# A decoder layer in float32 on one core: the softmax's row sums move from GpSimd and TensorE to ScalarE's accumulator, and VectorE writes the rounded query and key projections

## The reference

```
qkv = x @ attn_qkvw + attn_qkvb                      # q, k, v: 2 x 32 heads x 512 x 32
scores = einsum('bhqd,bhkd->bhqk', q, k) * (1 / sqrt(32))
probs = softmax(scores, axis=-1)
ctx = einsum('bhqk,bhkd->bhqd', probs, v)
x = layernorm(x + ctx @ attn_ow + attn_ob)
x = layernorm(x + fake_quant(x) @ fake_quant(ctx_4096))       # 1024 x 1024 per batch
x = layernorm(x + x @ W_base.T + b_base + experts(x))         # top 2 of 8 experts of rank 16
```

## Time and profile before

| | us |
|---|---|
| median of 3 runs | 793.83 (792.41 to 796.04) |
| profiled execution, span | 793.7 |
| TensorE (PE) busy | 745.3, 94% |
| VectorE (DVE) busy | 516.9, 65% |
| ScalarE (ACT) busy | 284.9, 36% |
| GpSimd (POOL) busy | 443.0, 56% |

### The profile page before, as it was taken

How to read it: one execution, slowest core, us unless ns; L and a number is a source line. 1 busy time by engine, 2 the same in 40 slices (tenths; PEclk the granted TensorE clock), 3 DMA queues, 4 the chain that set the end, 5 groups by cost and what they waited for, 6 DMA issues and landing times.

```text
span 793.7 us, 11643 instructions
## 1 busy us (share of the span) xinstructions
PE 745.3 (94%) x3688; PEld 533.3 (67%) x3688; DVE 516.9 (65%) x791; ACT 284.9 (36%) x443; POOL 443.0 (56%) x323
## 2 busy tenths in 40 slices
PE   5989999999999999999999998779999977999996
PEld 4758667668668668668667663257766756788884
DVE  4766558558558558558558567875667679466554
ACT  3214334334334334334334354613443481211111
POOL 4056597497587587587587467823453374112111
PEclk9999999999999999999999997989999998999999
DMA  7744325335334335335333644725354321122201
GB/s 253 252 113 163 105 71 172 104 73 168 104 76 164 103 77 165 103 76 165 103 75 89 186 142 117 246 83 205 107 163 134 126 82 53 41 93 82 76 27 53
DMA packets 50223, 95.10 MB, mean 120 GB/s; under 512 B 9744, under 2 KB 18448, under 8 KB 49296
## 3 DMA queue, kind: packets, MB, share of 16 engines
q1 hardware_dynamic: 50192, 94.72, 38.6%
HBM read 52.34 MB, written 16.78 MB: 87 GB/s over the span
## 4 chain that ended last, share of the span: by engine, by line
PE 58%; issue 16%; DVE 12%; POOL 4%; SPq 4%; DMA 4%; ACT 1%; POOLq 0%; DVEq 0%; ACTq 0%
PE bank L416 34%; PE bank L475 7%; PE bank L493 7%; PE bank L506 6%; SPq L224 3%; POOL xb L1023 2%; DVE st L1199 2%; PE bank L428 2%; DMA kp<-k_lo 2%; POOL mv L973 1%; DVE big_lo L1079 1%; DMA ctx_scratch<-ctxs 1%; DMA sc<-in_scales 1%; PE bank L444 1%; DVE x1s L1297 1%
## 5 line engine op out<-in xcount | busy, mean ns | idle before, releaser
L739 ACT ACTIVATE probs<-bank 128x512 f32<-128x512 f32 x256 | 152.3, 598 | 270.5 <-PE bank L493 269.6
L1128 DVE TENSOR_REDUCE m_col<-bank 128x1 f32<-128x512 f32 x256 | 171.3, 685 | 50.8 <-PE bank L475 47.9
L416 PE MATMUL bank<-big_hi,w_hi 128*128 128x512 f32 x384 | 156.1, 406 | 8.1 <-DVE big_lo L1051 6.8
L416 PE MATMUL bank<-big_lo,w_hi 128*128 128x512 f32 x384 | 152.8, 398 | 0.0
L416 PE MATMUL bank<-big_hi,w_lo 128*128 128x512 f32 x384 | 151.1, 394 | 0.0
L973 POOL TENSOR_TENSOR mv<-mv,consts 128x1 f32<-128x1 f32 x24 | 19.2, 799 | 173.1 <-DVE mv L1207 173.1
L937 POOL TENSOR_TENSOR psumk<-probs 128x512 f32<-128x512 f32 x64 | 84.8, 1325 | 54.0 <-ACT probs L739 49.0
L475 PE MATMUL bank<-kp,qp 96*128 96x512 f32 x256 | 104.8, 409 | 7.4 <-DMA kp<-k_lo 4.6
L493 PE MATMUL bank<-qp,kp 98*128 98x512 f32 x256 | 106.8, 418 | 0.4 <-ACT probs L739 0.4
L939 POOL TENSOR_TENSOR psumk<-psumk,probs 128x512 f32<-128x512 f32 x64 | 88.2, 1378 | 5.0
L416 PEld LDWEIGHTS bank<-big_hi,w_hi 128*128 128x128 f32 x384 | 73.3, 191 | 23.8 <-DVE w_lo L1042 6.0
(11 more groups left out here) (132 smaller groups left out, 1103.2 us busy)
## 6 DMA issues: line engine op xcount, KB each, us to landing
w_raw<-in_wqkv SPq DMA_DIRECT2D x7, 1536.0 KB, 6.7
c_raw<-in_ctx SPq DMA_DIRECT2D x16, 512.0 KB, 3.5
qp<-q_hi SPq DMA_DIRECT2D x128, 64.0 KB, 2.0
kp<-k_hi SPq DMA_DIRECT2D x128, 64.0 KB, 2.0
big_raw<-in_xT SPq DMA_DIRECT2D x16, 256.0 KB, 6.4
qp<-q_lo SPq DMA_DIRECT2D x64, 64.0 KB, 2.0
kp<-k_lo SPq DMA_DIRECT2D x64, 64.0 KB, 2.0
c_scratch<-c_q SPq DMA_DIRECT2D x16, 256.0 KB, 2.2
```

The lines of the kernel that those rows point to most:

```text
L416: mm = nc.tensor.matmul(dst, lhs[a], rhs[b], start=(k == 0 and n == 0) if first is None else False, stop=(k == last_k and n == 2))
L739: nc.scalar.activation(probs[:, j, t, :], bank(ST0 + i % 2), ACT.Exp, scale=SM_SCALE).then_inc(sem["exp_ok"], 1)
L1128: nc.vector.reduce_max(m_col[:, n:n + 1], bank(MAX0 + n % 2), AX).then_inc(sem["rowmax"], 1)
```

## The change

- `row_sums`, `add_keys`, the tiles `psumk` and `ones` go. Instead ScalarE runs an exponential over each block of the first scores (queries x keys), with the negated maximum as its bias, written back into the same bank, and with the accumulator output `accum_out` into a column of `l_col`: that is the sum of the row.
- VectorE takes the reciprocal of the 128x16 tile (`invert_sums`), TensorE transposes it (`recip_to_rows`, slot 6), VectorE copies it to `r_row` (`copy_recip`), SP stores it to DRAM and spreads it with four DMAs to 32 partitions each (`store_recip`, `spread_recip`). `divide` multiplies with `r_all` and runs when these have landed.
- The first scores rotate over three banks, start in slot 2 (`score_slot`), and a block waits for the sum of the block three before it. The bank of the row sums is one of the three; the maxima are transposed into PROJ0.
- VectorE rounds q and k (in front of the remainder, in `low`); ScalarE no longer does.
- The factor 1/sqrt(32) moves from the exponential to the weights and the bias of q. For group 0 VectorE rounds the q weights, for the others GpSimd scales them in place first.
- The maxima are taken negated, the rows in `kp` are 1 instead of -1. The constants of the quantisation are computed at the end of step 0. In the routing four semaphores become one.

```diff
+        def score_slot(n):
+            return 2 + (38 * n + 14) // 15
...
# SP
+            def store_recip(u):
+                wait_alone(sp, sem["r_row_ok"], u + 1)
+                if not isinstance(u, int) or u >= 1:
+                    wait_alone(sp, sem["r_in"], 16 * HPG * u)
+                sp.dma_start(r_d, r_row[:, :]).then_inc(sem["r_out"], 16)
+
+            def spread_recip(u):
+                wait_alone(sp, sem["r_out"], 16 * (u + 1))
+                if not isinstance(u, int) or u >= 1:
+                    wait_alone(sp, sem["ctx_ok"], u)
+                for j in range(HPG):
+                    sp.dma_start(r_all[j * HD:(j + 1) * HD, :], r_heads[j:j + 1, :].to_broadcast([HD, S])).then_inc(sem["r_in"], 16)
...
+                if finish:
+                    store_recip(s - 2)
                 if proj:
-                    sp.wait_ge(sem["lo_ok"], 2 * s + 1)
+                    wait_alone(sp, sem["lo_ok"], 2 * s + 1)
                     early = range(HPG if isinstance(s, int) and s < 2 else 2)
                     for j in early:
                         pack(s, par, j, "q")
-                    sp.wait_ge(sem["lo_ok"], 2 * s + 2)
+                if finish:
+                    spread_recip(s - 2)
+                if proj:
+                    wait_alone(sp, sem["lo_ok"], 2 * s + 2)
...
             store_context(UNITS - 2, 0, G - 1)
+            store_recip(UNITS - 1)
+            spread_recip(UNITS - 1)
             load_ow(1, 3 * UNITS)
...
# TensorE
-            def row_sums(u):
-                pe.wait_ge(sem["psum_ok"], HPG * (u + 1))
...
-                for j in range(HPG):
-                    mm = nc.tensor.matmul(banks[LSUM][j * HD:(j + 1) * HD, :], ones[:, :], psumk[:, j, :],
-                                          start=True, stop=True, skip_group_check=True)
-                mm.then_inc(sem["l_mm"], 1)
...
-                    if n >= 2:
-                        pe.wait_ge(sem["rowmax"], NS * (s - 1) + n - 1)
-                    nc.tensor.matmul(bank(MAX0 + n % 2), qp[0:SHIFT, 1 - par, j, t * P:(t + 1) * P],
+                    if n >= 3:
+                        pe.wait_ge(sem["sum_ok"], NS * (s - 1) + n - 2)
+                    elif n == 0 and (not isinstance(s, int) or s >= 2):
+                        pe.wait_ge(sem["sum_ok"], NS * (s - 1))
+                    nc.tensor.matmul(bank(MAX[n % 3]), qp[0:SHIFT, 1 - par, j, t * P:(t + 1) * P],
                                      kp[0:SHIFT, 1 - par, j, :], start=True, stop=True).then_inc(sem["max_mm"], 1)
...
+                def recip_to_rows():
+                    pe.wait_ge(sem["r_ok"], s - 1)
+                    if divides(s):
+                        pe.wait_ge(sem["ctx_ok"], s - 2)
+                    nc.tensor.transpose(banks[recip_bank(s)][0:NS, P:2 * P], r_col[:, :], ident[:, :]).then_inc(sem["r_mm"], 1)
...
-                    if maxima and done < NS and 15 * (q - FIRST_SCORE) >= 32 * done:
+                    if maxima and done < NS and q == score_slot(done):
...
-                    if divides(s) and q == 4:
-                        row_sums(s - 3)
+                    if finish and q == 6:
+                        recip_to_rows()
...
# ScalarE
+                def exp_scores(i):
+                    j, t = i // QT, i % QT
+                    act.wait_ge(sem["st_mm"], NS * (s - 2) + i + 1)
+                    if i == 0 and (not isinstance(s, int) or s >= 3):
+                        act.wait_ge(sem["pv_mm"], s - 2)
+                    nc.scalar.activation(probs[:, j, t, :], bank(ST0 + i % 2), ACT.Exp).then_inc(sem["exp_ok"], 1)
+
+                def exp_sum(n):
+                    act.wait_ge(sem["rowmax"], NS * (s - 1) + n + 1)
+                    nc.scalar.activation(bank(MAX[n % 3]), bank(MAX[n % 3]), ACT.Exp, bias=m_col[:, n:n + 1],
+                                         accum_out=l_col[:, 1 - par, n:n + 1]).then_inc(sem["sum_ok"], 1)
+
+                done = 0
+                for q in range(3, 3 * NS + 3):
+                    if finish and q % 3 == 0:
+                        exp_scores(q // 3 - 1)
+                    if maxima and done < NS and q == (score_slot(done) + 3 if proj else 3 * done + 3):
+                        exp_sum(done)
+                        done += 1
...
# GpSimd
+                if piece == 0:
+                    nc.gpsimd.tensor_scalar(w_raw[:, 0], w_raw[:, 0], SM_SCALE, 0.0, ALU.mult, ALU.add).then_inc(sem["w_scaled"], 1)
+                    wait_alone(pool, sem["w_scaled"], g_next)
...
-                nc.gpsimd.tensor_tensor(psumk[:, j, :], probs[:, j, 0, :], probs[:, j, 1, :], ALU.add).then_inc(sem["pool_sum"], 1)
...
# VectorE
             def divide(u):
-                dve.wait_ge(sem["l_mm"], u + 1)
-                nc.vector.reciprocal(recip[:, :], bank(LSUM)).then_inc(sem["recip_ok"], 1)
-                dve.wait_ge(sem["recip_ok"], u + 1)
+                dve.wait_ge(sem["r_in"], 16 * HPG * (u + 1))
+                dve.wait_ge(sem["pv_mm"], u + 1)
                 if not isinstance(u, int) or u >= 1:
                     dve.wait_ge(sem["ctx_out"], 16 * u)
-                nc.vector.tensor_tensor(ctxs[:, :], bank(context_bank(u)), recip[:, :], ALU.mult).then_inc(sem["ctx_ok"], 1)
+                nc.vector.tensor_tensor(ctxs[:, :], bank(context_bank(u)), r_all[:, :], ALU.mult).then_inc(sem["ctx_ok"], 1)
+
+            def invert_sums(u, q):
+                dve.wait_ge(sem["sum_ok"], NS * (u + 1))
...
+                nc.vector.reciprocal(r_col[:, :], l_col[:, q]).then_inc(sem["r_ok"], 1)
+
+            def copy_recip(u):
+                dve.wait_ge(sem["r_mm"], u + 1)
...
+                nc.vector.tensor_copy(r_row[:, :], banks[recip_bank(u + 2)][0:NS, P:2 * P]).then_inc(sem["r_row_ok"], 1)
...
                 def low(piece):
-                    dve.wait_ge(sem["hi_ok"], 2 * s + piece + 1)
+                    wait_alone(dve, sem["proj_done"], 3 * s + piece + 1)
+                    if not isinstance(s, int) or s >= 1:
+                        for h in range(HPG):
+                            wait_alone(dve, packed[h], PACK_INC * s)
+                    nc.vector.tensor_scalar(hi[:, :], bank(PROJ1 if piece == 0 else PROJ0),
+                                            bias[:, bass.ds(g, 1), piece:piece + 1].rearrange("p a b -> p (a b)"), None, ALU.add).then_inc(sem["hi_ok"], 1)
+                    wait_alone(dve, sem["hi_ok"], 2 * s + piece + 1)
                     nc.vector.scalar_tensor_tensor(lo[:, :], bank(PROJ1 if piece == 0 else PROJ0),
...
-                        nc.vector.reduce_max(m_col[:, n:n + 1], bank(MAX0 + n % 2), AX).then_inc(sem["rowmax"], 1)
-                    if proj and n in (3, 10):
-                        low(0 if n == 3 else 1)
+                        nc.vector.reduce_max(m_col[:, n:n + 1], bank(MAX[n % 3]), AX, negate=True).then_inc(sem["rowmax"], 1)
+                    if finish and n == 2:
+                        copy_recip(s - 2)
+                    if proj and n in (5, 11):
+                        low(0 if n == 5 else 1)
```

More of the change, by code:

```diff
@@ L584, in out_project @@
                         pe.wait_ge(sem["ow_lo"], h * KT + k + 1)
-                    if isinstance(n, int) and n == 0 and h == 0 and k == 5:
-                        row_sums(UNITS - 1)
                     if h and k == KT // 2 and (not isinstance(n, int) or n >= 1):
@@ L719, in _ @@
             split_x(0, range(KT))
[L720 removed]
+            act.wait_ge(sem["scale_q"], 1)
             def round_ow(h, k):
@@ new lines, in step @@
+                done = 0
[5 more added lines that the diff above has]
+                        done += 1
+                    if isinstance(s, int) and s == 0 and q in (16, 33):
+                        split_x(1, range(5) if q == 16 else range(5, KT))
+                    if isinstance(s, int) and s == UNITS - 1 and q % 3 == 0 and q // 3 > NS - KT:
+                        round_ow(0, q // 3 - 1 - (NS - KT))
+                    if isinstance(s, int) and s == UNITS + 1 and q == 21:
```

180 lines of the change are left out of this document (77 added, 103 removed).

## The result

The changed kernel takes 783.72 us (median of 4 runs, 783.35 to 786.72), the kernel before 794.88 us on the same chip (4 runs, 792.41 to 796.04): ratio 0.9879, 95% interval 0.9857 to 0.9902. It is faster, by 11 us instead of the 21 us forecast.

The account below looks back on a forecast made before the run. TensorE was taken as the bound, busy 387.93 of 388.00 us in the 13 steady steps; 793.7 less 12.2 (row sums), 8.2 (tail) and 0.5 (start) gave 772.8, so 773 us, range 766 to 786 us.

Parts of the forecast that it names:

- rival C: Both ends give nothing back (clock drop at the start, step 16's slower pairs, late output weights): 782 to 787 us, chance 0.11.
- Row sums off TensorE: Steps 3 to 15 lose 1.09 us of matmuls each, steps 2 to 15 gain a 0.14 us transpose: net 12.2 us gained.
- ScalarE, the doubtful part: Each accumulating sum on ScalarE costs 0.78 us, between 0.58 and 0.98; up to 0.95 costs TensorE nothing in steady steps.
- Rivals A and B: ScalarE's sums set the steady step: A, dearer than 0.95 us, 781 to 792 us, 0.13; B, slower than before, 0.09.
- VectorE's rounding: In each step VectorE gains two roundings of at most 0.75 us; its load goes from 19.4 to 18.0 us of 29.
- Step 16: In this step without projections, ScalarE's exponential and sum per pair take 1.27 us; context starts 3.5 us later.
- Steps 16 and 17 and the first tile: End of the attention: first output tile 5.1 us earlier, no row sums or slow start there, together 8.2 us gained.
- Start: Step 1: first score waits 3.2 us for its key pack, two later waits go, 0.5 us gained.
- Sum: Whole kernel: 793.7 - 12.2 - 8.2 - 0.5 = 772.8 us, the profiled span taken as the median of the runs.

Follow-up runs that it names:

- e16: The kernel before with all eight matmul passes of the row sums left out from the second unit on: 779.23 us (0.9821).
- e7: The changed kernel with the accumulator output of its sum exponentials left out, the sums being a constant: 782.66 us (0.9861).
- e8: The changed kernel with ScalarE again writing the rounded query and key projections, VectorE only the remainders: 794.94 us (1.0019).
- e15: The changed kernel with two more ScalarE copies of 128x512 a step into a spare tile that nobody waits for: 784.81 us (0.9890).
- e2: The changed kernel with the 2 MB load of the second half of the quantised context issued before step 16: 778.34 us (0.9802).
- e11: The changed kernel with the edits of e1 and e2, and the first tile's residual loaded ahead of the output weights' second half: 774.18 us (0.9740).
- e1: The changed kernel with VectorE taking the last group's reciprocal in front of the product of the group before: 777.15 us (0.9783).
- e9: The changed kernel with step 0's 1.5 MB weight load issued behind the key packs and the packed keys' memset on GpSimd: 782.63 us (0.9856).
- e10: e11 with the edits of e9 added: 770.58 us (0.9704).
- e13: The changed kernel with step 0's 1.5 MB weight load behind the key packs and the packed keys' memset as VectorE's first instruction: 783.05 us (0.9856).
- e14: e11 with the edits of e13 added: 771.41 us (0.9724).
- e12: The kernel before with six of the eight matmul passes of each row sum left out, except the first unit's: 793.02 us (0.9988).

## Why the prediction was off

It said 773.0 us; 783.7 came. The range of 766 to 786 holds that, but only by its share for rival C; the forecast of 768 to 777 missed. Faster was right, and so was the mechanism of the steady steps. The step that failed is the tail (steps 16 and 17 and the first tile): 8.2 us of gain forecast, 2.9 us of loss in the profiled execution. The start failed too: 0.5 us of gain forecast, 4.1 us of loss. The steps gave 3.6 us more than forecast and hid part of it.

- **Row sums off TensorE**, forecast 12.2 us in the 13 steps, measured 15.8: a term mis-sized, in the kernel's favour. I took 1.09 us for the group, but the interval behind it is stretched as well, 0.34 us instead of 0.23 (297.06 to the first row below); e16 gives 1.18 for the whole. The new transpose costs 0.11 and not 0.14. That is 1.07 of the 1.22 us a step. The last 0.15 us or so is a small pause that an interval of the kernel before showed (the other rows, 0.30 and 0.34 us apart) and this one doesn't have; that was only read, not tried. TensorE's timeline in the kernel before:

```profile
297.40 0.40 PE L416 MATMUL bank<-big_hi,w_hi 128*128 128x512 f32 x1
...
342.18 0.40 PE L416 MATMUL bank<-big_hi,w_lo 128*128 128x512 f32 x1
342.48 0.50 PE L475 MATMUL bank<-kp,qp 96*128 96x512 f32 x1
342.82 0.39 PE L493 MATMUL bank<-qp,kp 98*128 98x512 f32 x1
```

- **ScalarE, the doubtful part**: 0.78 us forecast, 0.67 measured (e7: 0.57 of it without the read). Rivals A and B did not occur. The rule of the Trainium skill (VectorE: DVE Perf Modes, Two Vector instructions with no wait between them) that an accumulator output is a second instruction, which it states of VectorE, holds on ScalarE here. The price that I worked out for that case, 0.78 to 0.98 us, was too high: it is 0.67, near my lower bound of 0.58.
- **VectorE's rounding**: I wrote that the new pair "holds up the next maximum by no more than before" and gave it no term. The bound of 0.75 us was right for each instruction. But with the sums on ScalarE this half is what makes the rest worth anything: without it the kernel is back at 794.9 us (e8), and by the hand-over, not the load (e15). The forecast was right that this half costs nothing and didn't see what it is worth.
- **Step 16**: pairs of 1.27 us forecast, 1.14 measured; from step 15's transpose to step 16's it grew by 2.06 us (21.78 to 23.84), less than I had thought.
- **Steps 16 and 17 and the first tile**, the step that failed: "a wait of 1.6 for the product" was put in the middle of step 17. The wait was 9.39 us, at its third score, with the slow clock behind it (granted clock 0.81 from 484.6 to 511.3 us). In the steady steps I had asked whether the new transpose waits for its reciprocal and found that "it doesn't wait"; for step 17 I didn't ask what the reciprocal is queued behind. I listed "product 0.7, correction 1.5, copy 0.3" and left out the reciprocal between product and correction, on which TensorE waits. And I read the 8.7 us of the store as a latency, where the load in front of it made up more than half (in the changed kernel 10.4 us with it, 4.3 without, e2). The product itself came about when I had it, 38.6 us after step 15's transpose against 37.5. Forecast from step 15's transpose to the first tile: 46.8 us; measured 55.5; with both causes removed 44.4 (e11). Step 17 itself I had 1.3 us too short: 10.7 us, where e11 takes 12.0 with only 0.4 us of wait in it.
- **Start**: 3.2 us of wait forecast, 6.2 in the profiled execution, 4.2, 4.2 and 6.4 in e1's, e2's and e11's, which have the same start. I left the clock out of the main line and had it only in rival C. Rival C's outcome, 782 to 787 us with both ends giving nothing back, is what came, partly by luck: it had the ends lose up to 5 us, they lost 7.0 in the profiled execution, and the steps gave more than its 12.2. Its mechanism was right at the start; in the tail it named step 16's pairs and the output weights, which weren't the cause.
- **Sum**: I laid the profiled span on the median of the runs. Where both are known, a run's time is 1.8 us over its span (786.72 and 784.9), so that the 793.7 us belong to an execution of some 795.5 us. The difference of 21 us isn't touched by it.

**What stays open.** Five edits at the start gained 0.2, 0.2, -2.0, 1.1 and 0.7 us alone, although in each the wait it aimed at went or shrank; the 95% intervals of all five overlap the changed kernel's. The start varies by itself: in four executions whose code is the same up to there (the changed kernel, e1, e2, e11), step 2's transpose comes between 80.92 and 84.87 us; it comes at 81.85 in e9 and 78.91 in e10, and at 80.55 in e13 and 78.28 in e14, again with the same start. One profile a version can't tell a gain of 2 us there. With the tail mended, e9's edits gave 3.6 us in the same session and e13's 2.8 us across two sessions (1.3 us by the ratios to the kernel before), which isn't clear of the noise. So a chain of several items of nearly equal length (pack, memset, packs and rounding, clock) is likely but not shown, and how much each is worth isn't settled.

## What to carry to other kernels

When an instruction on the bound engine is added, follow its operand back through the other engine's queue in every stage, the irregular last steps above all: a reciprocal of 0.24 us held the bound engine for 9.4 us because it stood behind an instruction that waited for a transfer, and putting it first gave 6.6 us. When work is moved to an engine, look at the hand-overs as well as the load: two more copies a step on ScalarE cost nothing, two roundings there on which VectorE's queue waits cost 10 us. And where the forecast rests on a wait that goes away, name the next two items behind it before counting the gain.

## What the runs showed of the hardware

- Matmuls of 32 output columns, placed on four different column groups, overlap: eight passes on four groups took 0.99 us to the next start and two passes on one took 0.97. The matmul behind them delays its follower by another 0.1 us. Leaving out part of the group (e12) gained nothing, all of it 1.18 us a step (e16).
- ScalarE's accumulator output is an instruction of its own, 0.21 us long in its row and 0.10 us in the queue, behind an exponential of 128x512.
- A clip of 128x1024 on VectorE took 4.01 us instead of 0.69 beside a GpSimd memset of 3.51 us.
- A store of 256 KB was waited for 10.4 us behind a 2 MB load, and 4.3 us when that load was issued a step earlier.
- The clock behind a wait, over all kernels here: after each of the waits of 2.6 to 9.4 us that TensorE had from step 1 up to 526 us, its matmuls started 0.43 us apart, the 1.2 GHz level, at once or a few matmuls later (7 to 13 of them behind the waits for the first pack). After waits of 1.6 to 2.5 us it went either way: the clock fell in e16 (1.65 us, at 49.29) and held in e12 (2.48 us, at 36.16) and e8 (2.37 us, at 35.24). After the waits of 1.2 us in the kernel before it held. The length of the wait alone doesn't decide it. It also fell without such a wait: 0.53 in step 16 of the changed kernel.
